# Two adjacency layers in one sweep: column 0 of row blocks 2 to 15 summed during row block 1

## The reference

```python
keep = (u >= 0.1);  x_drop = x * keep / 0.9
x = layernorm(x + adj @ x_drop)                      # layer 0
x_proj = tanh(|x|) * x / (|x| + eps)                 # norm clipped to 0..10
support = adj @ x_proj                               # layer 1
out = arctanh(|support|) * support / (|support| + eps)   # norm clipped to 0..0.999
x = layernorm(x + out @ kernel + bias)
```

## Time and profile before

| what | value |
|---|---|
| time, median of 3 runs | 987.54 us |
| span of the profiled execution, first to last instruction | 983.9 us |
| what lies around the span, against the median | 3.6 us |
| PE busy | 936.0 us, 95% of the span |
| DVE, ACT, POOL busy | 268.9, 53.4, 57.0 us |
| bytes moved by DMA | 353.02 MB, mean 359 GB/s |
| block loads | 330, median 9.8 us from issue to landing |

### The profile page before, as it was taken

The page is one execution under the profiler, slowest core; times in us unless marked ns, Lnnn a source line. Parts: engine busy times, 40 slices in busy tenths (PEclk is TensorE's granted clock), DMA queues, the critical chain, the costliest instruction groups (busy, mean ns, idle before and its releaser), DMA issues.

```text
span 983.9 us, 8773 instructions
## 1 busy us (share of the span) xinstructions
PE 936.0 (95%) x3392; PEld 362.2 (37%) x3392; DVE 268.9 (27%) x886; ACT 53.4 (5%) x138; POOL 57.0 (6%) x49
## 2 busy tenths in 40 slices
PE   4678999999999999999999999999999999999994
PEld 1122333334343434343434444344343443434441
DVE  1120212214041312312131111301204013066775
ACT  0000000000000000000000000000000000002233
POOL 0000000000000000000000000000000000002332
PEclk9999999999999999999999999999999999999997
DMA  9999999998989899989599895997988989999980
GB/s 369 414 422 420 421 421 422 378 424 347 405 302 424 338 422 356 409 335 377 189 370 422 329 350 203 343 422 267 392 289 318 418 289 381 348 380 420 420 361 32
DMA packets 52743, 353.02 MB, mean 359 GB/s; under 512 B 6368, under 2 KB 8416, under 8 KB 10464
## 3 DMA queue, kind: packets, MB, share of 16 engines
q1 hardware_dynamic: 49824, 350.25, 89.5%
q10 hardware_dynamic: 2880, 2.23, 0.7%
HBM read 350.36 MB, written 2.10 MB: 358 GB/s over the span
## 4 chain that ended last, share of the span: by engine, by line
PE 81%; DMA 12%; SPq 3%; DVE 2%; ACT 1%; POOL 0%; issue 0%; ACTq 0%; POOLq 0%; DVEq 0%
PE sums_both L543 41%; PE sums_part L524 19%; PE sums_first L524 16%; DMA ring<-adj_dram 12%; PE turned L524 2%; SPq L283 2%; PE turned L575 1%; PE sums_both L585 1%; ACT xres L335 1%; PE sums_first L585 1%; SPq L278 1%; DVE stats L394 0%; POOL rooted L300 0%; DVE y L484 0%; SPq L279 0%
## 5 line engine op out<-in xcount | busy, mean ns | idle before, releaser
L543 PE MATMUL sums_both<-ring,feats 128*128 128x512 f32 x960 | 424.5, 597 | 2.3 <-DMA ring<-adj_dram 2.2
L524 PE MATMUL sums_first<-ring,feats 128*64 128x512 f32 x1088 | 249.0, 601 | 31.1 <-DMA ring<-adj_dram 31.0
L543 PEld LDWEIGHTS sums_both<-ring,feats 128*128 128x128 f32 x960 | 178.4, 190 | 238.0 <-issue 230.5
L524 PE MATMUL sums_part<-ring,feats 128*64 128x512 f32 x896 | 201.3, 596 | 0.0
L524 PEld LDWEIGHTS sums_first<-ring,feats 128*64 128x64 f32 x1088 | 75.8, 137 | 197.6 <-issue 137.3
L403 DVE TENSOR_TENSOR row_saved<-sums_both,row_saved 64x512 f32<-64x512 f32 x15 | 10.2, 683 | 389.7 <-ACT row_saved L351 389.7
L524 PEld LDWEIGHTS sums_part<-ring,feats 128*64 128x64 f32 x896 | 64.8, 136 | 130.6 <-issue 130.2
L441 DVE TENSOR_TENSOR support<-sums_part,support 64x512 f32<-64x512 f32 x86 | 58.8, 684 | 156.1 <-PE sums_part L524 156.0
L310 POOL TENSOR_TENSOR rooted<-base,power 128x8 f32<-128x8 f32 x16 | 27.8, 1738 | 842.2 <-DVE base L414 842.2
L442 DVE TENSOR_TENSOR support<-sums_part,support 64x512 f32<-64x512 f32 x87 | 60.4, 694 | 3.0
L351 ACT COPY row_saved<-sums_first 128x512 f32<-128x512 f32 x16 | 9.4, 587 | 725.4 <-PE sums_first L524 725.4
(11 more groups left out here) (54 smaller groups left out, 173.7 us busy)
## 6 DMA issues: line engine op xcount, KB each, us to landing
ring<-adj_dram SPq DMA_DIRECT2D x330, 1024.0 KB, 9.8
xres<-x_dram SPq DMA_DIRECT2D x8, 256.0 KB, 15.9
support<-u_dram SPq DMA_DIRECT2D x8, 256.0 KB, 16.0
out_dram<-xres ACTq DMA_DIRECT2D x16, 128.0 KB, 6.8
sel<-selector_dram ACTq DMA_DIRECT2D x1, 32.0 KB, 3.3
selw<-selector_dram ACTq DMA_DIRECT2D x1, 32.0 KB, 3.7
selw<-weight_dram ACTq DMA_DIRECT2D x1, 32.0 KB, 6.2
bias_sb<-bias_dram ACTq DMA_DIRECT2D x1, 32.0 KB, 6.6
```

The lines of the kernel that those rows point to most:

```text
L524: last = nc.tensor.matmul(bank[at:at + F], feats[:, c * TB + t, which, :], ring[:, uses[i][0], t, :], start=start and t < 2, stop=stop and ...
L543: last = nc.tensor.matmul(sums_both[r % 2][:], feats[:, c * TB + t, :, :], ring[:, slot, t, :], start=c == 0 and t == 0, stop=c == r - 1 a ...
```

## The change

Blocks (r, 0) for r = 2 to 15 are no longer the first step of their row. They become steps of a new kind, `early`, placed in row 1 after the `part` of column 0: three `early`, three of row 1's remaining steps, and so on. There are 14 of them. Their loads move with them; the number of loads stays 330 and the number of matmuls is unchanged.

An `early` step sums into `sums_both[0]` (even r) or `turned[1]` (odd r), waits until the step two before it in the same bank has been saved, and ACT empties the bank with three copies: the layer 1 half into `support` of row r, and the layer 0 half in two pieces into `feats[..., 1, :]` of row r, a place that is unused until the row is mapped. In rows 2 to 15 `both` begins with column 1. The ACT copy of `support` (L353) remains for row 1 only. At the end of these rows DVE adds the two saved pieces onto `row_saved` (two additions of 64 x 256), adds the `sums_both` half as before, and adds the layer 1 half onto `support` (64 x 512). The `turn` of row 1 now stands behind the last two `early` steps and one `first` step.

```diff
--- before.py
+++ after.py
@@ -39,6 +39,7 @@
 
 TURN_AFTER = 1
 COLUMN_AFTER = 5
+EARLY_RUN = 3
 FINISH_EVERY = 5
 GROUP = 2
 
@@ -86,8 +87,17 @@
         return steps
 
     for r in range(NB):
-        blocks = [("both", r, c) for c in range(r - 1)]
+        blocks = [("both", r, c) for c in range(r >= 2, r - 1)]
         blocks += [("first", r, c) for c in range(r + HELD[r], NB)]
+        if r == 1:
+            early = [("early", row, 0) for row in range(2, NB)]
+            order += blocks[:TURN_AFTER] + [("turn", 0)] + blocks[TURN_AFTER:COLUMN_AFTER] + column(0)
+            rest = blocks[COLUMN_AFTER:] + [("both", 1, 0)] + [("hold", 1, c) for c in range(HELD[1], 0, -1)]
+            while early:
+                order += early[:EARLY_RUN] + rest[:EARLY_RUN]
+                early, rest = early[EARLY_RUN:], rest[EARLY_RUN:]
+            order += rest
+            continue
         if r:
             order += blocks[:TURN_AFTER] + [("turn", r - 1)] + blocks[TURN_AFTER:COLUMN_AFTER]
             order += column(r - 1)
...
@@ -183,7 +192,7 @@
 
     def saved_through(r):
 
-        return 1 + 2 * r
+        return min(1 + 2 * r, 2 + r)
 
     with ExitStack() as es:
         def sb(name, shape):
@@ -224,6 +233,12 @@
         turned = [ps(f"turned{i}") for i in range(2)]
 
         part_banks = sums_part + turned
+        early_banks = [sums_both[0], turned[1]]
+
+        def early_sums(r):
+
+            at = feats[:, r * TB:(r + 1) * TB, 1, :]
+            return at[0:F], at[F:P]
 
         projected = [[bank[:].rearrange("p (t f) -> p t f", t=TB) for bank in pair]
                      for pair in (sums_both, sums_first)]
@@ -236,6 +251,8 @@
         row_summed = sem("row_summed")
         row_sums_saved = sem("row_sums_saved")
         row_joined = sem("row_joined")
+        early_saved = sem("early_saved")
+        support_begun = sem("support_begun")
         row_turned = sem("row_turned")
         rows_projected = sem("rows_projected")
         turned_read = sem("turned_read")
@@ -341,15 +358,24 @@
                                   xres[:, r * TB:(r + 1) * TB, :]).then_inc(out_stored, 16)
 
             k = 0
-            for step in order:
+            for i, step in enumerate(order):
                 r = step[1]
+                if step[0] == "early":
+
+                    low, high = early_sums(r)
+                    bank = early_banks[r % 2]
+                    act.wait_ge(block_released, uses[i][2])
+                    nc.scalar.copy(support[half(r), r // 2], bank[F:P])
+                    nc.scalar.copy(low, bank[0:F, 0:BS // 2].rearrange("p (t f) -> p t f", f=F))
+                    nc.scalar.copy(high, bank[0:F, BS // 2:BS].rearrange("p (t f) -> p t f", f=F)
+                                   ).then_inc(early_saved, 1)
                 if step[0] == "hold" and step[2] == r:
 
                     act.wait_ge(row_summed, r + 1)
                     if r:
                         act.wait_ge(row_turned, r)
                     nc.scalar.copy(row_saved[:], sums_first[r % 2][:]).then_inc(row_sums_saved, 1)
-                    if r:
+                    if r == 1:
                         nc.scalar.copy(support[half(r), r // 2], sums_both[r % 2][F:P]).then_inc(row_sums_saved, 1)
                 if step[0] == "turn":
                     act.wait_ge(norm_ready, r + 1)
@@ -399,8 +425,19 @@
 
             def layer1_join(r):
 
-                dve.wait_ge(row_sums_saved, saved_through(r) - 1)
+                dve.wait_ge(row_sums_saved, 2 if r == 1 else saved_through(r))
+                if r == 1:
+                    V.tensor_tensor(row_saved[0:F], sums_both[1][0:F], row_saved[0:F], ALU.add).then_inc(row_joined, 1)
+                    return
+                low, high = early_sums(r)
+                saved = row_saved[:].rearrange("p (h t f) -> p h t f", h=2, f=F)
+                dve.wait_ge(early_saved, r - 1)
+                V.tensor_tensor(saved[F:P, 1], saved[F:P, 1], high, ALU.add)
+                done(V.tensor_tensor(saved[0:F, 0], saved[0:F, 0], low, ALU.add))
                 V.tensor_tensor(row_saved[0:F], sums_both[r % 2][0:F], row_saved[0:F], ALU.add).then_inc(row_joined, 1)
+                total = support[half(r), r // 2]
+                V.tensor_tensor(total, sums_both[r % 2][F:P], total, ALU.add).then_inc(support_begun, 1)
+                dve.wait_ge(support_begun, r - 1)
 
             def layer1_end(r):
                 rows = slice(r * TB, (r + 1) * TB)
@@ -532,17 +569,28 @@
                     c = step[2]
                     slot, nth, _ = uses[i]
                     pe.wait_ge(block_loaded[slot], 16 * nth)
+                if kind == "early":
+                    if r >= 4:
+                        pe.wait_ge(early_saved, r - 3)
+                    pe.wait_ge(mapped, c + 1)
+                    for t in range(TB):
+                        last = nc.tensor.matmul(early_banks[r % 2][:], feats[:, t, :, :], ring[:, slot, t, :],
+                                                start=t == 0, stop=t == TB - 1)
+                    last.then_inc(block_released, 1)
                 if kind == "both":
-                    if c == 0 and r >= 2:
-
-                        pe.wait_ge(row_sums_saved, saved_through(r - 2))
-                        if r > 2:
-                            pe.wait_ge(row_joined, r - 2)
+                    begin = c == (r >= 2)
+                    if begin and r == 2:
+                        pe.wait_ge(early_saved, NB - 2)
+                    if begin and r == 3:
+                        pe.wait_ge(row_sums_saved, saved_through(1))
+                        pe.wait_ge(row_joined, 1)
+                    if begin and r >= 4:
+                        pe.wait_ge(support_begun, r - 3)
                     pe.wait_ge(mapped, c + 1)
                     for t in range(TB):
                         last = nc.tensor.matmul(sums_both[r % 2][:], feats[:, c * TB + t, :, :],
                                                 ring[:, slot, t, :],
-                                                start=c == 0 and t == 0, stop=c == r - 1 and t == TB - 1)
+                                                start=begin and t == 0, stop=c == r - 1 and t == TB - 1)
                     last.then_inc(block_released, 1)
                 if kind in ("first", "hold"):
                     start = c == (r + HELD[r] if r + HELD[r] < NB else NB - 1)
```

## The result

The changed kernel takes 978.95 us (median of 4 runs, 978.22 to 981.03) against 987.16 us (4 runs of the kernel before): ratio 0.9918, 95% interval 0.9904 to 0.9932. In a second set it took 978.6 against 987.62 us, ratio 0.9911 (0.9898 to 0.9925). So it gains 8 to 9 us; 9.1 were forecast, and 978.4 us as the time. The profiled execution took 978.45 us and has a span of 976.3 us, 7.6 less than before. Only 2.15 us lie around this span. Before the change 3.6 us were put there, from the median and the span of one execution.

What follows compares the result with a forecast made beforehand. PE was taken to set the pace for most of the span, the load stream at the start; 11.2 - 1.8 - 0.25 = 9.1 us gained, 987.5 - 9.1 = 978.4 us, range 976.6 to 982.3.

Steps and rivals of the forecast that it cites:

- What bounds the early rows: Turn 0 to turn 3: narrow passes are bound by their loads, wide ones by PE; 11.2 us lost.
- What the move fills: Rows 1 to 3: row 1 gains 8.0 us of load lead, waits in rows 2 and 3 go; 1.8 us stays.
- the low point of the lead: Just ahead of the wide pass before turn 3: load lead down to 1.6 us, 2.6 with the first early load's lead.
- The first rival: Rows 2 and 3: a load waits as the lead runs out, 4.7 us given back, 983.1 us; chance 10%.
- The 0.25 us at turn 1: Turn 1 waits once for ACT's copies from the last early step's bank: 0.25 us, bounds 0 and 0.7.
- DVE at each row end: Turns 2 to 15: two new additions leave 0.7 us of 1.6 us spare, so cost 0.
- the rival of slower row ends: Turns 2 to 15: longer DVE chain makes turns late; 992 us if each addition took 1.3 us; chance 2%.
- No wait beyond 0.3 us: Sign expected at the turns: no wait there longer than 0.3 us.
- The price of a pass: PE without waits, from two stretches: 3.52 us for a wide pass, 1.75 us for a narrow one.
- wide passes above 3.52 us in row 1: Sign against the forecast: wide passes in row 1 taking more than 3.52 us.
- The sum: Whole kernel: 11.2 - 1.8 - 0.25 = 9.1 us gained, span 974.8 us, time 978.4 us.
- The rules weighed: Two skill rules, loads bound at 358 GB/s and PE idling under PSUM bank cycling; the trace was said to show neither.

Runs made afterwards that it cites:

- experiment 1: Kernel before, but from the 18th load on the block loads of rows 1, 2 and 3 bring only two of four K tiles; 976.46 us, ratio 0.9881.
- experiment 2: Changed kernel's bookkeeping without the move: column 0 stays an early step at the head of its own row; 987.75 us against 987.44, ratio 1.0003.
- 8: Changed kernel with one early step and one narrow pass in turn instead of threes; 980.74 us, ratio 0.9922.
- 10: Changed kernel with early steps in one run, column 0's part step one narrow pass earlier, two narrow passes ahead of turn 15; 978.42 us, ratio 0.99.
- 11: Changed kernel with early steps in one run and DVE adding the saved pieces onto the PSUM bank after the row's last wide pass; 977.91 us, ratio 0.9907.
- 7: Changed kernel with all 14 early steps in one run instead of threes between the narrow passes; 978.48 us, ratio 0.9907.
- Experiment 4: Changed kernel with two more DVE additions of 64 x 512 in each early row's end, ahead of the last one; 988.01 us, ratio 0.9999.

## Why the prediction was right

*What bounds the early rows: right.* The loss of 11.2 us and its cause, the loads, are confirmed by experiment 1, and experiment 2 shows that the gain comes from the place of the blocks alone.

*What the move fills: right, but for the low point of the lead.* Turn 1 was put at 143.9 us, turn 2 at 178.0; the trace has 143.77 and 178.03. The 25 loads against 15 wide and 10 narrow passes, the lead and its use in rows 2 and 3 hold also for 7 and 11 blocks. The lead was thin, as said, but its low point was put at the wrong place. It was put just ahead of turn 3, and from turn 3 to turn 4 the lead was to grow again. In 1, 8, 10 and 11 a load wait of about 0.5 us stands ahead of turn 4. Behind turn 3 thirteen of the 17 slots hold blocks for later, and SP waits up to 12.0 us for a slot to come free: in the changed kernel DMA moves 210 GB/s from 214 to 219 us and 280 from 219 to 224, instead of 421. The sum over loads and work left this stop out. The changed kernel has no wait there in two traces; of 7 and 11, which have the same order of steps, one has it and one has not. So the lead is near zero there. The first rival, that the lead runs out, did not come about in the changed kernel; in 8, 10 and 11 the one wait made turn 3 to turn 4 longer by 0.8 to 1.2 us.

*The 0.25 us at turn 1: not there.* The last early step's bank was free in time, since ACT's last copy ended at 143.34 and the turn began at 143.77; from the narrow pass to turn 1 are 1.87 us, as from the pass ahead of turn 0 before the change (58.35 to 60.22). ACT's three copies take 582, 366 and 364 ns.

*DVE at each row end: right for 13 turns, wrong for one.* At turns 2 to 14 the weights are loaded 0.75 us after the last addition ends; 0.7 was reckoned. Experiment 4 shows that some 0.4 us more are spare, since the matmul follows a late weight load more closely; the rival of slower row ends counted without them. The step said that the place is each turn from 2 to 15 with a wide pass as cover. Turn 15 has a narrow one, which the order of steps shows, and the wait of 0.74 us there was priced at 0. "No wait beyond 0.3 us" failed at this place.

*The price of a pass: one number for two things.* Two equations gave 3.52 us for a wide pass as a mean. A wide pass taken out of a run of wide ones gives back only 3.43 us: nine of the ten stretches from turn 4 to turn 14 became shorter by 3.42 to 3.45 us, one by 3.79. In threes it costs 3.50 as a mean, and 3.63 between narrow ones (83.35 to 86.98). The prediction named wide passes above 3.52 us in row 1 as a sign against it; some are, by up to 0.02 us. The ten stretches gave 34.7 us instead of 35.2. The stretches from turn 0 to turn 4 took 193.6 us, where 193.1 were worked out. Together about 1 us.

*The sum: in part luck.* 9.1 - 0.8 (turn 15 and its stretch) - 0.5 - 0.5 = 7.3 us from turn 0 to turn 15; the two traces show 805.39 - 797.95 = 7.44. So the span was forecast at 974.8 us and came out 1.5 us longer, at 976.3. The forecast of 978.4 us held because the 3.6 us around the span, taken from a median and another execution's span, were 2.15 in the profiled execution of the changed kernel: two errors of about 1.5 us cancelled. Over 44 executions of the kernel before, 2.1 to 3.4 us lie around the span, 2.7 as a mean; over eight of the changed kernel 2.1 to 2.2. The medians differ by 8.2 and 9.0 us, more than the two traces. The kernel before has a median span of 984.9 us over these executions, 1.0 above its trace, and the changed one 976.45, so part of the difference is that the trace before is one of the shorter ones; part, about 0.6 us, lies around the span, and no run shows why. The time of turn 0 alone scatters from 59.3 to 63.1 us over all the traces here.

*The rules weighed.* Loads ran at 420 to 422 GB/s from turn 0 to turn 3 before the change and at 420 to 421 from turn 0 to turn 2 after it. So the trace does not agree with the 358 GB/s of the Trainium skill ("DMA: Bandwidth & Descriptors", section "Where 436 GB/s comes from"), with this one core at work. Switching banks with each wide pass costs nothing that shows: 3.43 us per pass at clock 1.00 in one run of 14, the same as a pass taken out of a run in one bank. The effect that the Trainium skill describes ("TensorE: Matmul & The Clock Gate", section "A second HAM failure mode: psum-queue depth-cycling") does not appear.

## What to carry to other kernels

Where one stage waits for loads and later ones for PE, work that uses a load for longer can be moved from the later to the early stage; its worth is the table of loads against work, stage by stage, and it ends where the two are level. Follow the lead stretch by stretch together with the free buffers, since it stops growing when they are all held. Check the cover of a lengthened chain at every place where it occurs, the last one above all, since the order often differs there. A wait that is taken away comes back wherever the next stream is only just ahead, so mend one place at a time and read the stretch times, not the total.

## What the runs showed of the hardware

A turn that was held up lost less than its chain was late: with the chain 0.8 us past the point at which the weights are usually loaded, the matmuls began 0.37 us late. In the row ends undisturbed, the weight load stands 0.43 us ahead of its matmul; when late, it was followed by the matmul after 0.03 us (857.89 and 857.92). So here the spare time ahead of a turn reached nearly to the matmul's start, not only to its weight load.

After a wait of 1.4 us ahead of turn 15, in one kernel's trace, PE's granted clock was 0.50 for some 3.5 us, and the six `part` passes there took 1.6 us longer. After waits of 0.7 us (five traces) and of 2.1 us (one) at the same place it stayed at 1.00. A wait of PE can so cost twice its length, or nothing more; what decides it no run here shows.

A change between wide passes (stationary operand of 128 columns) and narrow ones (64 columns on each half of the array) cost 0.3 to 0.35 us there and back, while a change of PSUM bank cost nothing that shows.
